# Weights of the second layer loaded in the last batch of the first, products of the identity in three gaps of TensorE, and both orders of steps rewritten

## The chip, the core and the metric

The kernel runs on one core of one Trainium2 chip. The metric is the device time of one execution in microseconds. In the texts PE is TensorE, DVE is VectorE, ACT is ScalarE, POOL is GpSimd and SP is SyncE, whose only work is to issue transfers. ACT issues transfers as well.

## The reference

Two layers are applied one after the other to an input of 16 batches, each of 512 tokens by 128 features. Each layer normalizes its input and adds to it an attention part and a part with experts.

```
x  = L0_attn_x                                    # 16 x 512 x 128
xn = layernorm(x)
x  = x + attention_0(xn) + soft_experts(xn)       # layer 1
xn = layernorm(x)
x  = x + attention_1(xn) + routed_experts(xn)     # layer 2
```

- attention_0 has 16 heads of 8 features, a latent of 128 for keys and values, a rotary part of 32, and a causal softmax.
- soft_experts forms logits of the tokens against 8 x 64 slot vectors (themselves normalized), softmaxes them over the tokens for what goes into the slots and over the slots for what comes out, and runs 8 experts (128 to 512 to 128, gelu).
- attention_1 has 16 heads of 64 features and a causal softmax over the 512 tokens of a batch.
- routed_experts has 16 experts and one shared one, each 128 to 128 to 128 with silu. Of the 16 the best 8 by sigmoid score are kept for each token.

## The kernel before

Each layer is one block of the program (`layer0`, `layer1`), in which every engine has a stream of its own. Between the blocks all engines meet. The intermediate x goes through a tensor in HBM, `x1_scratch`.

Within a layer the work of a batch is cut into named steps: `norm`, `scale` and `xnT` (layer norm and turning it), `q`, `k`, `r`, `v`, `max` (scores for the row maximum, a masked product), `turn_max`, `exp` (scores again, with the maximum taken off by a row in the product), `values`, `turn_rows` and so on, and for the experts `logits_s`, `logits_c`, `dispatch`, `slots`, `hidden`, `expert_out`, `combine` in the first layer and `gate_in`, `up_in`, `hw`, `down` in the second. A table written out by hand, `ORDER0` or `ORDER1`, says in which order the steps of one batch stand among those of the next and the last (the number behind the name: `("norm", 1, 0)` is the norm of the next batch). `layer0_program` and `layer1_program` repeat the table for each batch, and every engine walks through the same list and does its part of each step. An engine never goes on to a later step while it waits in an earlier one.

PE writes into eight banks of PSUM. Four are a ring for everything (`ps_any`, handed out by `Banks`, which gives a step the bank that was filled longest ago, so that a step waits until the step that held the bank has been emptied), the others hold the scores for the exponential (`ps_exp`), the sums over values (`ps_out`) and in the second layer the sums of the exponentials (`ps_sum`).

At the start of the first layer SP issues 18 loads of weights and constants and then x of the first batch, and ACT issues w1, b1, w2 and eight loads of b2. DVE and POOL normalize the slot vectors (`slot_n`), PE turns them into `snT`, and only then does the list of steps begin. At the start of the second layer SP issues 11 loads and x, ACT issues seven. ACT and DVE split every weight into a high and a low half in 16 bits (`low_weights`): four before the first step, and the three expert matrices `w_g`, `w_u`, `w_d` together before the first `gate_in`, for which PE waits:

```
                if at == first_expert:
                    pe.wait_ge(weights_lo, len(split_in) + len(split_late))
                    pe.wait_ge(late_loaded, all_late)
```

In the second layer a causal mask is added to scores by a product of its own behind each piece of scores: 128 columns by `ident_h` and `mask_h` in `exp`, and two halves of 64 columns for each of two heads by `later_h` and `ident_2` in `max`. `max`, `values` and `sums` use part of the array at a time (64 rows, 64 columns, 32 columns), other products all of it.

## Time and profile before

| what | value |
|---|---|
| median of 3 runs | 3098.85 us (3097.3 to 3101.01) |
| profiled execution | 3096.49 us, its span 3094.8 us |
| clock granted to TensorE, mean of the span | 0.984 of full |
| first layer, from the first instruction to the last product | 0 to 1157 us |
| second layer | 1161 to 3095 us |

The span runs from the first to the last instruction, and 1.7 us lie around it. A full clock of TensorE is 2.4 GHz, a granted clock of 0.5 is 1.2 GHz. PE is busy for 93% of the span, but this figure is made of pipelined products with modelled ends, so that short gaps between groups of products do not show in it.

### The profile page before, as it was taken

The numbers are of one execution on the slowest core, as the hardware profiler recorded it, in microseconds if no ns is written. First come the engines' busy times: TensorE is split into PE (matmuls) and PEld (weight loads), VectorE is DVE, ScalarE is ACT, GpSimd is POOL, SyncE is SP. The second block draws the span as 40 slices with busy tenths as digits, with TensorE's granted clock in tenths as the row PEclk, the third lists the DMA queues.
The fourth block names the chain that finished last, engine by engine and source line by source line (L and its number), as shares of the span: only waits on it lengthen the run. The fifth ranks groups of instructions, "written<-read, shape, count | busy, mean of one in ns | idle before, by whom it ended". The sixth has DMA issues, their size and how long they took to land.

```text
span 3094.8 us, 63911 instructions
## 1 busy us (share of the span) xinstructions
PE 2884.3 (93%) x23492; PEld 1512.2 (49%) x23492; DVE 2310.2 (75%) x4199; ACT 1802.6 (58%) x3771; POOL 1314.4 (42%) x1223
## 2 busy tenths in 40 slices
PE   3999999999999984999999999999999999999997
PEld 1555555555555551444444444444444444444443
DVE  4777777777777755778878878878778778778874
ACT  2777766667776763555555555555555555555543
POOL 0433333333333321544544554554554554544543
PEclk8999999999999996999999999999999999999998
DMA  4222222222222214444444444444444444444442
GB/s 112 59 57 54 53 72 68 54 59 56 59 52 61 68 29 131 117 119 115 120 122 116 120 122 115 121 121 115 123 119 116 122 120 115 126 117 115 118 120 69
DMA packets 271910, 297.70 MB, mean 96 GB/s; under 512 B 30832, under 2 KB 235760, under 8 KB 271088
## 3 DMA queue, kind: packets, MB, share of 16 engines
q1 hardware_dynamic: 249936, 276.88, 35.2%
q10 hardware_dynamic: 21664, 16.73, 1.7%
q8 instruction: 189, 3.10, 0.4%
q14 instruction: 121, 0.99, 0.1%
HBM read 141.46 MB, written 25.69 MB: 54 GB/s over the span
## 4 chain that ended last, share of the span: by engine, by line
PE 51%; DMA 3%; DVE 3%; issue 2%; SPq 2%; ACT 1%; POOL 0%; DVEq 0%; ACTq 0%; POOLq 0%
PE l_ps_out L1643 8%; PE l_ps_any L1543 6%; PE l_ps_any L1545 6%; PE l_ps_any L1544 6%; PE l_ps_any L1668 5%; PE l_ps_exp L1626 4%; PE l_ps_any L1675 4%; PE l_ps_exp L1628 4%; PE l_ps_any L1601 3%; DMA l_y_rec<-rec_scratch 2%; PE l_ps_sum L1654 2%; PE l_ps_exp L1630 2%; SPq L1173 1%; DVE l_neg_max L1466 1%; PE l_ps_any L1606 1%
## 5 line engine op out<-in xcount | busy, mean ns | idle before, releaser
L1260 POOL TENSOR_TENSOR l_hid<-l_hid,l_spread 128x512 f32<-128x512 f32 x256 | 327.9, 1281 | 655.1 <-DVE l_hid L1495 480.3
L1347 ACT ACTIVATE l_probs<-l_ps_exp 128x512 f32<-128x512 f32 x640 | 376.8, 595 | 211.4 <-PE l_ps_exp L1630 201.0
L673 DVE TENSOR_REDUCE neg_max<-ps_any 128x1 f32<-128x384 f32 (+3 forms) x704 | 411.0, 634 | 115.7 <-PE ps_any L800 113.7
L536 ACT ACTIVATE probs<-ps_exp 128x512 f32<-128x512 f32 x640 | 352.1, 607 | 41.5 <-PE ps_exp L815 28.4
L455 POOL TENSOR_SCALAR_AFFINE_SELECT probs<-probs 128x512 f32<-128x512 f32 x256 | 160.0, 637 | 458.9 <-ACT probs L536 457.4
L1466 DVE TENSOR_REDUCE l_neg_max<-l_ps_any 128x2 f32<-128x768 f32 (+2 forms) x384 | 316.1, 862 | 35.4 <-PE l_ps_any L1606 34.4
L1626 PE MATMUL l_ps_exp<-l_q_a,l_k_a 128*128 128x512 f16 (+3 forms) x1024 | 306.4, 300 | 10.3 <-DMA l_q_b<-l_max_row 6.5
L1643 PE MATMUL l_ps_out<-l_probs,l_v 128*64 128x512 f32 (+3 forms) x2048 | 303.9, 439 | 0.7 <-ACT l_yT L1322 0.7
L1499 DVE TENSOR_TENSOR l_hw<-l_hid,l_hw 128x512 f16<-128x512 f32 x272 | 257.9, 953 | 60.2 <-ACT l_hw L1330 60.0
L1353 ACT ACTIVATE l_hid<-l_ps_any 128x512 f32<-128x512 f32 x272 | 162.4, 597 | 236.3 <-PE l_ps_any L1545 217.9
L1628 PE MATMUL l_ps_exp<-l_q_b,l_k_b 65*128 65x512 f16 (+3 forms) x1024 | 295.2, 300 | 0.0
L798 PE MATMUL ps_any<-k_st,q_st 120*128 120x128 f16 (+3 forms) x1024 | 254.4, 304 | 30.6 <-DMA k_st<-stack_scratch 12.1
L1242 POOL TENSOR_TENSOR l_key_sum<-l_probs 128x768 f32<-128x768 f32 x128 | 232.4, 1815 | 0.0
L815 PE MATMUL ps_exp<-q_st,k_st 121*128 121x512 f16 (+3 forms) x1024 | 223.9, 302 | 4.7 <-DMA q_st<-max_row 4.2
L1489 DVE SCALAR_TENSOR_TENSOR l_hid<-l_hid,l_ps_any 128x512 f32<-128x512 f32 x272 | 185.3, 681 | 51.7 <-ACT l_hid L1353 47.4
L1495 DVE TENSOR_TENSOR l_hid<-l_ps_any,l_hid 128x512 f32<-128x512 f32 x272 | 186.3, 685 | 41.5 <-PE l_ps_any L1545 33.6
L1643 PEld LDWEIGHTS l_ps_out<-l_probs,l_v 128*64 128x64 f32 x2048 | 135.7, 136 | 162.4 <-issue 139.0
L1330 ACT ACTIVATE l_hw<-l_hid 128x512 f16<-128x512 f32 x272 | 167.3, 621 | 78.6 <-POOL l_hid L1260 62.4
L1630 PE MATMUL l_ps_exp<-l_mask_h,l_ident_h 128*128 128x128 bf16 x1024 | 212.3, 219 | 0.0
L1247 POOL TENSOR_TENSOR l_key_sum<-l_key_sum,l_probs 128x512 f32<-128x512 f32 x128 | 171.6, 1341 | 70.0 <-ACT l_probs L1347 63.0
L800 PE MATMUL ps_any<-mask_h,ident_h 128*128 128x128 bf16 x1024 | 196.6, 221 | 0.0
L1322 ACT ACTIVATE l_yT<-l_ps_out 128x512 f32<-128x512 f32 x128 | 76.1, 595 | 202.4 <-PE l_ps_out L1643 202.4
(262 smaller groups left out, 6731.5 us busy)
## 6 DMA issues: line engine op xcount, KB each, us to landing
l_spread<-route_scratch SPq DMA_DIRECT2D x128, 512.0 KB, 4.7
l_q_a<-l_q_hi SPq DMA_DIRECT2D x256, 128.0 KB, 2.4
l_y_rec<-rec_scratch SPq DMA_DIRECT2D x128, 256.0 KB, 4.3
l_q_b<-l_q_lo SPq DMA_DIRECT2D x128, 128.0 KB, 2.4
l_k_a<-l_k_hi SPq DMA_DIRECT2D x128, 128.0 KB, 3.2
l_k_a<-l_k_lo SPq DMA_DIRECT2D x128, 128.0 KB, 2.8
l_k_b<-l_k_hi SPq DMA_DIRECT2D x128, 128.0 KB, 2.9
q_st<-rot_hi SPq DMA_DIRECT2D x64, 128.0 KB
```

The lines of the kernel that those rows point to most:

```text
L536: nc.scalar.activation(probs[:, n % 2, u], ps_exp[:, (10 * g + u) % 3], ACT.Exp, scale=float(HD0 + DR) ** -0.5).then_inc(exp_done.sem, 1)
L673: nc.vector.tensor_reduce(neg_max[:, n % 2, heads[0]:heads[0] + k, t], src, AX.X, ALU.max, negate=True).then_inc(drained["dve"], 1)
L798: pe.matmul(out, q_st[0:K_MAX0, n % 2, h, t * P:t * P + P], k_st[0:K_MAX0, n % 2, h, 0:w], start=True, stop=False)
L1242: nc.gpsimd.tensor_tensor(s[:, :, P:T], u[:, 0:2, P:T], u[:, 2:4, 0:3 * P], ALU.add).then_inc(added.sem, 1)
L1260: nc.gpsimd.tensor_tensor(at, at, spread[:, c % 3, n % SPREAD], ALU.mult).then_inc(weighted.sem, 1)
L1347: nc.scalar.activation(probs[:, n % 2, u], ps_exp[:, (5 * p + u) % ST_BANKS], ACT.Exp, scale=float(HD1) ** -0.5).then_inc(exp_done.sem, 1)
L1466: ins = nc.vector.tensor_reduce(maxima[:, :, q, t], scores[:, :, c:c + (t + 1) * P], AX.X, ALU.max, negate=True)
L1499: nc.vector.tensor_tensor(hw[:, k % HW_SLOTS, 1], hid[:, k % HID_SLOTS], hw[:, k % HW_SLOTS, 0], ALU.subtract).then_inc(hw_ok.sem, 1)
L1626: pe.matmul(out, k_a[:, g % 2, h, k * P:k * P + P], q_a[:, g % 2, h, k * P:T], start=True, stop=False)
L1628: pe.matmul(out, k_b[0:K_B, g % 2, h, k * P:k * P + P], q_b[0:K_B, g % 2, h, k * P:T], start=False, stop=False)
L1630: ins = pe.matmul(out[:, 0:P], ident_h[:], mask_h[:], start=False, stop=True)
L1643: ins = pe.matmul(ps_out[HD1 * r:HD1 * r + HD1, k * P:T], v[:, k, h * HD1:h * HD1 + HD1], probs[:, n % 2, u, c:c + T - k * P], start=(k == ...
```

## The change

- **Start.** SP issues x of the first batch first, then 8 loads. The other ten go onto ACT's queue, ahead of w1, b1 and w2. The eight loads of b2 are issued by SP at the third `load_heads`. The slot vectors are normalized and turned in a new step `snT`, which stands eight steps ahead of the first logits. POOL, not DVE, clears `v_aug`. `squares` shares its place with `slot_n`.
- **Between the layers.** A class `Early` holds memory that both layers use (`stage`, `ident`, `bias`, `x_in` of the second layer). 14 loads of second-layer weights are issued by ACT in the last batch of the first layer, one ahead of each of the last 14 exponentials, and x of batch 0 by SP at the last `load_heads`. ACT no longer waits for the last store of the first layer at the end of its block. Only w_u, w_d and w_out are loaded at the start of the second layer. The splitting of weights is spread over steps: w_d, above all, only at the first `hw`. POOL clears `k_b`.
- **Products of the identity.** PE multiplies the identity by itself (128 x 128, 32 bits, into a bank that the next user overwrites) 8 times when its first loads have come, 24 times ahead of the first `max`, and 20 times at the start of the second layer.
- **Masks of the second layer.** The masks of an `exp` or `max` step with two pieces are added by one product over both pieces.
- **Sums of the second layer.** The first `sums` of a set of four waits for the reciprocals of the set just before it, not of the one before that.
- **Both tables** `ORDER0` and `ORDER1` are rewritten. They hold the same steps.

```diff
+SPIN_START, SPIN_STACK, SPIN_TURN = 8, 24, 20
 ORDER0 = (
-    ("exp", 0, 0, 4), ("logits_s", 0, 0), ("exp", 0, 0, 5), ("exp", 0, 0, 6), ("soft_s", 0, 0),
+    ("exp", 0, 0, 1), ("attnT", -1, 0), ("exp", 0, 0, 2), ("max", 0, 1, 5), ("exp", 0, 0, 3), ("max", 0, 1, 6),
...
+    first = min(steps.index(x) for x in (("logits_s", 0, 0), ("logits_c", 0, 0)))
+    return steps[:first - 8] + [("snT", 0, 0)] + steps[first - 8:]
...
+            sp.dma_start(x_in[:], a["L0_attn_x"][0].rearrange("(t p) d -> p t d", p=P)).then_inc(x_loaded.sem, 16)
             for dst, src in loads:
                 sp.dma_start(dst, src).then_inc(loaded, 16)
...
+                if name == "load_heads" and (b, n) == (0, 2):
+                    for dst, src in b2_loads:
+                        sp.dma_start(dst, src).then_inc(late_loaded, 16)
+                if name == "load_heads" and (b, n) == (batches - 1, G - 1):
+                    sp.wait_ge(stored.sem, stored.at(0, 16))
+                    sp.dma_start(early.x_in[:], x1_dram[0].rearrange("(t p) d -> p t d", p=P)
+                                 ).then_inc(early.x_loaded.sem, 16)
...
+            for dst, src in act_loads:
+                act.dma_start(dst, src).then_inc(act_loaded, 16)
             act.dma_start(w1_in, a["L0_ffn_w1"].rearrange("e d h -> d e h")).then_inc(w1_loaded, 16)
...
+                    k = len(early.loads) - (G - n) * len(EXP0) + u if b == batches - 1 else -1
+                    if k >= 0:
+                        act.dma_start(*early.loads[k]).then_inc(early.loaded, 16)
                     nc.scalar.activation(probs[:, n % 2, u], ps_exp[:, (10 * g + u) % 3], ACT.Exp,
...
-            act.wait_ge(stored.sem, stored.at(batches, 0))
...
+            def spin(count):
+
+                for _ in range(count):
+                    pe.matmul(ps_exp[:, 2, 0:P], ident[:], ident[:], start=True, stop=True)
+
+            spin(SPIN_START)
...
+                if at == first_max:
+                    spin(SPIN_STACK)
+                    pe.wait_ge(prep, 3)
...
+                if at == first_hw:
+                    act.wait_ge(down_loaded, 32)
+                    high_weights(split_late[1:])
+                    act.wait_ge(weights_lo, len(split_in) + 1)
+                if name == "xnT" and b == 0:
+                    high_weights(split_in[4:])
...
-                        ins = pe.matmul(out[:, 0:P], ident_h[:], mask_h[:], start=False, stop=True)
-                    ins.then_inc(exp_full.sem, 1)
+                    out = ps_exp[:, m % ST_BANKS].rearrange("p (x q) -> p x q", q=P)
+                    pe.matmul(out[:, diagonals([c for r, k, c in EXP1[step[3]]])], ident_h[:],
+                              mask_h[:, 0:len(EXP1[step[3]])], start=False, stop=True
+                              ).then_inc(exp_full.sem, 1)
...
-                    if j == 0 and p >= 2 * SET:
-                        pe.wait_ge(rec_ok.sem, rec_ok.at(p // SET - 1, 0))
+                    if j == 0 and p >= SET:
+                        pe.wait_ge(rec_ok.sem, rec_ok.at(p // SET, 0))
```

The order of instructions shows three places. The first is DVE at the start of the program, before the change (`slot_nat`, `slot_n`, `snT` belong to the slot vectors, `BN_STATS` is the norm of the first batch):

```order
L572 MEMSET v_aug 128x2048
L573 MEMSET k_st 32x4096
L577 ISA squares,slot_ss<-slot_nat 128x128
...
L580 TENSOR_SCALAR slot_sm<-slot_ss 128x4
L583 SCALAR_TENSOR_TENSOR slot_n<-slot_nat,slot_r,slot_gamma 128x128 x4
L585 CAST ident_h<-ident 128x128
...
L591 TENSOR_TENSOR snT<-ps_any,snT 128x512
L603 BN_STATS stats<-x_in 128x6 x4
```

and after it, with the same engine:

```order
L601 MEMSET k_st 32x4096
L636 BN_STATS stats<-x_in 128x6 x4
L640 BN_AGGR mv<-stats 128x2 x4
L642 TENSOR_SCALAR var_eps<-mv 128x4
L648 TENSOR_SCALAR xn<-x_in,mv,rstd 128x128 x4
L626 CAST ident_h<-ident 128x128
L627 CAST mask_h<-mask 128x128
...
L607 ISA slot_n,slot_ss<-slot_nat 128x128
...
L610 TENSOR_SCALAR slot_sm<-slot_ss 128x4
L613 SCALAR_TENSOR_TENSOR slot_n<-slot_nat,slot_r,slot_gamma 128x128 x4
L618 SCALAR_TENSOR_TENSOR snT<-ps_any,snT 128x512
```

The norm of the first batch now stands ahead of all work on the slot vectors, which begins at row 34 of this engine's stream where it began at row 3. The second place is DVE at the start of the second layer, before the change (`l_w_...` are the low halves of split weights, `l_score` begins the choice of experts):

```order
L1362 MEMSET l_k_b 64x4096
...
L1369 CAST l_ident_h<-l_ident 128x128
...
L1379 SCALAR_TENSOR_TENSOR l_w_kvd<-l_probs,l_w_kvd 128x128
...
L1379 SCALAR_TENSOR_TENSOR l_w_kvu<-l_probs,l_w_kvu 128x2048
L1433 BN_STATS l_stats<-l_x_in 128x6 x4
...
L1386 SCALAR_TENSOR_TENSOR l_xn_p<-l_ps_any,l_xn_p 128x512
L1395 TENSOR_SCALAR l_score<-l_th 128x64
...
L1379 SCALAR_TENSOR_TENSOR l_w_g<-l_yT,l_w_g 128x2176
L1379 SCALAR_TENSOR_TENSOR l_w_u<-l_hw,l_w_u 128x2176
L1379 SCALAR_TENSOR_TENSOR l_w_d<-l_hid,l_w_d 128x2176
```

and after it:

```order
L1415 MEMSET l_ones_in 128x128
...
L1489 BN_STATS l_stats<-l_x_in 128x6 x4
...
L1495 TENSOR_SCALAR l_var_eps<-l_mv 128x4
...
L1434 SCALAR_TENSOR_TENSOR l_w_q<-stage,l_w_q 128x1024
L1501 SCALAR_TENSOR_TENSOR l_shift<-l_mv,l_rstd 128x4
L1434 SCALAR_TENSOR_TENSOR l_w_kvu<-stage,l_w_kvu 128x2048
L1422 CAST l_ident_h<-ident 128x128
...
L1441 SCALAR_TENSOR_TENSOR l_xn_p<-l_ps_any,l_xn_p 128x512
L1434 SCALAR_TENSOR_TENSOR l_w_g<-stage,l_w_g 128x2176
L1450 TENSOR_SCALAR l_score<-l_th 128x64
...
L1434 SCALAR_TENSOR_TENSOR l_w_u<-l_hw,l_w_u 128x2176
...
L1434 SCALAR_TENSOR_TENSOR l_w_d<-l_yT,l_w_d 128x2176
```

Four splits and the clearing of `l_k_b` stood ahead of the norm, now none does, and the three expert matrices stand apart from each other. The third place is PE inside the second layer, one `exp` and one `max` step with two pieces each, before the change:

```order
L1626 MATMUL l_ps_exp<-l_q_a,l_k_a 128x384
L1628 MATMUL l_ps_exp<-l_q_b,l_k_b 128x384
L1630 MATMUL l_ps_exp<-l_mask_h,l_ident_h 128x128
L1626 MATMUL l_ps_exp<-l_q_a,l_k_a 128x128
L1628 MATMUL l_ps_exp<-l_q_b,l_k_b 128x128
L1630 MATMUL l_ps_exp<-l_mask_h,l_ident_h 128x128
...
L1601 MATMUL l_ps_any<-l_k_hi,l_q_hi 128x384 x2
L1606 MATMUL l_ps_any<-l_ident,l_later_h 128x64 x4
L1601 MATMUL l_ps_any<-l_k_hi,l_q_hi 128x128 x2
L1606 MATMUL l_ps_any<-l_ident,l_later_h 128x64 x4
```

and after it:

```order
L1705 MATMUL l_ps_exp<-l_q_a,l_k_a 128x384
L1707 MATMUL l_ps_exp<-l_q_b,l_k_b 128x384
L1705 MATMUL l_ps_exp<-l_q_a,l_k_a 128x128
L1707 MATMUL l_ps_exp<-l_q_b,l_k_b 128x128
L1710 MATMUL l_ps_exp<-l_mask_h,l_ident_h 128x2x128
...
L1678 MATMUL l_ps_any<-l_k_hi,l_q_hi 128x384 x2
L1678 MATMUL l_ps_any<-l_k_hi,l_q_hi 128x128 x2
L1685 MATMUL l_ps_any<-l_ident,l_later_h 128x2x64 x4
```

The two mask products behind the pieces of one `exp` step have become one over 2 x 128 columns, and the eight small ones of a `max` step four over 2 x 64 columns.

## Rows read from the trace of the kernel before

**Rows 1.** The page: busy time of each engine

```profile
PE 2884.3 (93%) x23492; PEld 1512.2 (49%) x23492; DVE 2310.2 (75%) x4199; ACT 1802.6 (58%) x3771; POOL 1314.4 (42%) x1223
```

**Rows 2.** Busy time by stretch: length, then busy us and count of each engine, clock granted to PE as a share, DMA share, GB/s

```profile
52.60:76.00 23.40, 17.60 (x101) 9.51 (x102) 17.75 (x25) 10.04 (x15) 0.64 (x1) 0.69 0.15 33
110.00:1100.00 990.00, 935.28 (x8981) 550.83 (x8980) 739.56 (x1661) 695.21 (x1682) 351.24 (x377) 1.00 0.24 60
1157.20:1189.00 31.80, 0.04 (x1) 0.00 (x0) 10.68 (x27) 4.81 (x8) 1.14 (x2) 0.53 0.53 198
1189.00:1211.40 22.40, 9.05 (x38) 3.77 (x38) 13.70 (x28) 10.70 (x12) 0.00 (x0) 0.58 0.42 100
1211.40:1230.00 18.60, 15.63 (x88) 6.05 (x89) 13.69 (x20) 6.02 (x12) 5.08 (x4) 0.75 0.09 24
1230.00:3000.00 1770.00, 1740.69 (x12957) 854.89 (x12955) 1396.11 (x2202) 972.34 (x1807) 881.85 (x764) 1.00 0.47 119
```

**Rows 3.** Timeline of the start: start, us, engine, line, what [idle before <- releaser]

```profile
0.80 0.40 SPq L381 DMA_DIRECT2D ident<-in_ident  x1
...
11.14 4.93 SPq L381 DMA_DIRECT2D w_kr<-in_L_attn_W_k_rope  x3
16.11 1.02 SPq L388 DMA_DIRECT2D x_in<-in_L_attn_x  x1
...
23.13 0.29 DVE L577 CUSTOM_DVE_ANT_0 squares<-slot_nat 128x128 f32<-128x128 f32 x1 [15.69 <-DMA w_kr<-in_L_attn_W_k_rope]
...
29.57 0.86 DVE L603 BATCH_NORM_STATS2 stats<-x_in 128x6 f32<-128x128 f32 x4
...
34.76 0.60 ACT L469 ACTIVATE xnT<-ps_any 128x512 f32<-128x512 f32 x1 [5.91 <-PE ps_any L738]
...
52.62 0.29 PE L798 MATMUL ps_any<-k_st,q_st 120*128 120x128 f16 x1 [11.23 <-DMA k_st<-stack_scratch]
```

**Rows 4.** Transfers of the first 60 us: size of one and median us to landing

```profile
x_in<-in_L_attn_x SPq DMA_DIRECT2D x1, 256.0 KB, 7.5
```

**Rows 5.** PE's waits from 200 to 1000 us: us in total, times, longest

```profile
PE ps_any L798 <- ACT hT L553: 8.4, 22, 0.5
PE ps_any L738 <- ACT y_un L543: 8.1, 11, 0.7
PE ps_any L738 <- DVE xn L615: 8.1, 12, 0.7
```

**Rows 6.** PE's waits from 1300 to 3000 us

```profile
PE l_ps_any L1601 <- DVE l_neg_max L1466: 6.7, 9, 1.7
PE l_ps_exp L1626 <- DMA l_q_b<-l_max_row: 6.5, 5, 1.6
```

**Rows 7.** Timeline between the layers

```profile
1158.10 0.37 ACTq L567 DMA_DIRECT2D x_scratch<-x  x1
...
1161.75 3.47 DVE L1362 MEMSET l_k_b<- 64x4096 f16 x1 [3.69 <-PEq L205]
```

**Rows 8.** The chain of waits between the layers: start, us, what

```profile
1182.00 2.29 DVE l_w_kvu L1379
...
1202.33 1.91 ACT l_w_g L1279
1204.27 2.42 DVE l_w_g L1379
```

**Rows 9.** PE's waits between 1189 and 1230 us

```profile
PE l_ps_any L1543 <- DVE l_w_d L1379: 9.7, 1, 9.7
```

**Rows 10.** Timeline of PE around one set of value products in layer two

```profile
2009.11 0.22 PE L1630 MATMUL l_ps_exp<-l_mask_h,l_ident_h 128*128 128x128 bf16 x1
2009.25 2.38 PE L1643 MATMUL l_ps_out<-l_probs,l_v 128*64 128x512 f32 x16
2011.56 0.39 PE L1543 MATMUL l_ps_any<-l_xn_p,l_w_u 128*128 128x512 f16 x1
```

**Rows 11.** DVE's reciprocals of the sums, all 64

```profile
L1478 DVE RECIPROCAL l_rec<-l_ps_sum x64: 886/918/958, 1291.5 to 3070.4; 128x128 f32<-128x128 f32 x64
```

More of the change, by code:

```diff
@@ L383, in _ @@
                 n = which[0]
-                if name == "load":
+                if name == "load" and b:
                     if b:
@@ L472, in _ @@
                 n = which[0]
+                if name == "snT":
+                    nc.scalar.activation(snT[:, 0], full(act, "snT0"), ACT.Copy).then_inc(snT_hi, 1)
                 if name in ("xnT", "ckv"):
@@ L596, in low_part @@
                                                       op0=ALU.mult, op1=ALU.subtract)
-            for name, b, *which in program:
+            for at, (name, b, *which) in enumerate(program):
                 n = which[0]
+                if at == after_scale:
+                    dve.wait_ge(loaded, all_loaded)
+                    dve.wait_ge(act_loaded, all_act)
+                    nc.vector.tensor_copy(ident_h[:], ident[:]).then_inc(prep, 1)
+                    nc.vector.tensor_copy(mask_h[:], mask[:]).then_inc(prep, 1)
+                if name == "snT":
+                    slots_normed()
+                    bank = full(dve, "snT0")
+                    dve.wait_ge(snT_hi, 1)
+                    low_part(bank, snT, 1.0).then_inc(drained["dve"], 1)
                 if name == "norm":
@@ L955 @@
+    ("values", 0, 7), ("max", 1, 1, 0), ("max", 1, 1, 1), ("sums", 0, 7),
 )
@@ L1523, in _, with spin @@
         def _(pe):
-            pe.wait_ge(loaded, all_loaded)
-            pe.wait_ge(prep, 12)
-            pe.wait_ge(weights_lo, len(split_in))
+            def spin(count):
+                for _ in range(count):
+                    pe.matmul(ps_exp[:, ST_BANKS - 1, 0:P], ident[:], ident[:], start=True, stop=True)
+            spin(SPIN_TURN)
+            pe.wait_ge(early.loaded, early.all)
             def bank(name):
```

416 lines of the change are left out of this document (235 added, 181 removed).

## The prediction

> **What bounds the kernel now.** I read the page first, then busy time by stretch, then PE's waits in each stretch, and last the timeline and the chain of waits where a stretch is not full. The page gives PE 93% and no other engine over 75% [rows 1]. By stretch this is two full layers with gaps around them: PE is busy for 935 of the 990 us from 110 to 1100, and for 1741 of the 1770 us from 1230 to 3000, at the full clock in both [rows 2]. In these two stretches time can come only from fewer products, from closer products, or from PE's waits. The waits are small: in 800 us of the first layer 8.4 us for a bank that the gelu holds, 8.1 for `y_un`, 8.1 for the normalized x [rows 5]; in 1700 us of the second 6.7 for row maxima and 6.5 for the row of maxima that is brought by a transfer [rows 6].
>
> The gaps are different. At the start the reader should see three rows: x is issued only at 16.11, behind 18 other issues; DVE waits 15.69 us for the last weight and begins with the slot vectors at 23.13, and the norm begins at 29.57; the copy of xnT starts at 34.76, and the first scores at 52.62 [rows 3]. Between the layers PE does nothing from 1157.2 to 1189.0 while transfers run [rows 2], then works at a granted clock of 0.58, and waits 9.7 us for the last of the expert weights [rows 2, 9].
>
> **Start.** x is now issued at 0.80, where `ident` was. Its transfer took 7.5 us among others [rows 4], so it is there by 8.3 at the latest. The norm to the copy of xnT took 34.76 - 29.57 = 5.2 us [rows 3]. DVE would allow the copy at 13.5 or before. ACT must first issue 13 transfers: at the 0.40 us of `ident` this is 5.2 us, at the 4.93/3 = 1.64 us of `w_kr` it is 21 us [rows 3]. The issues that were slow stood behind a full queue, so I take 1.0 us for each of six short rotary pieces and 0.6 for the rest, 10 us in all, with a table load and the last landing at 14. The gain at xnT is 34.8 - 14 = 21 us, with bounds 12 and 26. From xnT to the first scores lie the same products, splits and transfers as before, 52.6 - 34.8 = 17.9 us [rows 3]; loads of w1 and w2 now run into them. I take 20.
>
> Given back: the slot work, on DVE from 23.13 to 29.57 [rows 3], comes later, in a stretch in which DVE is busy for 17.8 of 23.4 us and PE for 17.6 [rows 2]. What is not waiting in it is about 4 us of DVE. Also eight issues of b2 stand in SP's queue before the second row of maxima, 8 x 0.4 = 3.2 us [rows 3]. Hidden both cost nothing, on the path 7. I take 2.5. The 24 products of the identity fill a gap of 11.23 us [rows 3]; the stretch behind it ran at a clock of 0.69 [rows 2]. If the clock stays full, at most 17.6 x 0.31 = 5 us come back. 24 products of 128 columns in 32 bits end long before the stacks come, so I take 1.5. **Start: -20 + 2.5 - 1.5 = -19.**
>
> **Last batch of the first layer.** 14 issues on ACT, 14 x 0.4 = 5.6 us by the row of `ident`, each behind a wait for scores and ahead of an exponential. ACT is busy for 695 of 990 us [rows 2], so most of it is covered; without cover PE waits for a bank of scores each time. **+2**, bounds 0 and 5.6.
>
> **Between the layers.** Without the wait for the store the block ends some 2 us sooner: it is issued at 1158.10, and DVE's first instruction of the next layer starts at 1161.75 [rows 7]. Say DVE starts at 1159.8. Short clears 0.5, norm 1.6. ACT meanwhile issues 5 transfers (2.5) and converts four weights (3.2), which lasts until 1165.0. Scaling x (1.65), turning (1.1), the high half of w_g ahead of the copy (1.91, as in [rows 8]), copy and low half (1.3) give 1171 for what stood at 1191.6. That is 20.5 us. Now w_g's low half stands before the choice of experts, 2.42 us [rows 8], which leaves 18. The wait of 9.7 us for three matrices [rows 9] shrinks to w_u's conversion, 1.91 + 2.4 = 4.3 [rows 8]: 5.4 more. w_d's 4.3 comes later, on an ACT and a DVE that are busy for 6.0 and 13.7 of 18.6 us [rows 2]: half of it on the path, 2. The clock in 1189 to 1230 was 0.58 and 0.75 over 24.7 us of busy PE [rows 2], at most 7.7 us; the 20 products end some 5 us after the block starts and the next product is due about 8 us after it, so the clock may hold. I take 3.5, since DVE is nearly full too. **-18 - 5.4 + 2 - 3.5 = -25**, bounds -17 and -32.
>
> The Trainium skill (DMA: Bandwidth & Descriptors, "Issuing engines are not separate DMA queues") says that transfers of all engines share the same 16 DMA engines and that several issuers save only issue time. By it alone the start would gain little. The trace agrees in so far as DVE waits until 23.13 us for the last small load [rows 3]; but what PE waits for is the order of the bytes, and x and the weights of the first products come first now.
>
> **Steady part, first layer.** Same steps, other order. Distances in "us of products" below are counted from the two tables, a column as a cycle of 2.4 GHz (four in 32 bits), as are the changes of the array's shape. In the new table `values` (32 columns of the array), `r` and `expert_out` are more often neighbours: 23 changes between parts of the array and all of it per batch against 26. Such a change costs about 0.1: a mask product at 2009.11 ends its 0.05 of columns at 2009.16, and the value products behind it start at 2009.25 [rows 10]. Three fewer in each of 16 batches are 5 us. The wait for the normalized x (8.1 in 800 us, 0.7 a batch) should go, since 3.3 us of products now stand between `scale` and `xnT`, where 1.0 stood; `y_un` likewise (0.86 before, 1.9 now for the worst). `hidden` banks are reused after 1.45 us three times, as tight as before. In full that is 5 + 2 x 0.7 x 15 = 26 us. A new order opens waits that I can't see, so I take half. **-12**, bounds -26 and +10.
>
> **Steady part, second layer.** Masks: 8 products per pair of heads become 5, and 32 per group 20, with the same columns. What a product costs beyond its columns these rows don't show; I put it at 2 ns, so that 384 + 768 fewer are worth 2 us, with nothing and 10 us as ends. Changes of the array's shape go from 58 to 61 a batch, +5 us. The row of maxima has 3.8 us of products before its use at the tightest place against 2.3: some of the 6.5 us [rows 6]. **-1**, bounds -12 and +16.
>
> The skill (TensorEngine Tiling (Array Packing), "Key Properties") says that a change of tiling mode drains the engine. The gap of 0.09 us in rows 10 agrees. By that rule alone the tables would give -5 and +5, together nothing.
>
> **Sum.** -19 + 2 - 25 - 12 - 1 = -55 on the profiled execution's 3096.5 is 3041.5. The median of the runs shown is 2.4 above that execution, so I say **3044**.
>
> **Rivals.**
> - *The tables do more than I count.* An order chosen for this program takes out most remaining waits in both layers: 26 in the first, 12 in the second. 3044 - 14 - 11 = 3019. For it: every wait of rows 5 is of the kind an order can move. Against it: the tightest reuses of banks are alike in both.
> - *The tables cost.* `sums` of a new set waits for the reciprocals of the set before. They take 2 x 0.92 us [rows 11] on DVE, and only 4.3 us of products stand between the last `sums` of one batch and the first of the next, where 10.2 stood. DVE has a reduction of about 1.3 us before them, so some 3.3 us are needed on an idle DVE; a lag of 2 us costs 1 us a batch. With the 5 us of array changes, 13 above my sum, and no gain in the first layer, 12: 3069.
> - *The gaps give half.* Loads and stacks of the start collide, and DVE with its 14 us of conversions sets the pace between the layers. -9 and -13: 3066.
> - *Slower.* The same wait for reciprocals, with DVE late by 5 us: PE then loses 3.9 us twice a batch. It decides from 55/30 = 1.8 us for each of 30 sets. The other set has 14.5 us of products, so both would have to fail; DVE is busy for 1396 of 1770 us [rows 2], which leaves room: above 3105.
> - *The identity does nothing* for the clock: +5, inside my range.
>
> **How the numbers follow.** My forecast 0.55 (its own range 3028 to 3058), better tables 0.19, costly tables 0.11, half the gaps 0.12, slower 0.03. The range takes all but the ends: 3018 to 3068. A measurement of this kernel tells about 0.2% (6 us) from no change. The gaps alone give some 40 us, so faster 0.96, same 0.01, slower 0.03.
>
> **What would show it.** xnT's copy at 12 to 17 us and first scores at about 33; a granted clock of 1.0 from 33 to 56 if the products of the identity work. No transfer of weights on the path after the first layer's end; the turning of x within 9 us of the block's start; a wait of PE for w_u under 5 us, none for w_d. In the stretches, PE's idle share below 5.5% in the first layer, and rows for xn and `y_un` gone. I am wrong if PE waits for `l_rec`, if ACT issues its loads slowly at the start, or if the step `snT` shows as a hole.

## The result, and the profile after

The changed kernel takes **3175.78 us** (median of 4 runs, 3173.21 to 3181.64); the kernel before, 3098.76. The ratio is 1.0251, 95% interval 1.0233 to 1.0268: slower by 77 us where I forecast 55 us less. The profiled execution took 3174.8 us, with a span of 3173.1. Groups 0 to 3 below are the four groups of four heads that a batch has in either layer, each with its own `turn_max`; "the row" of a group is the row of maxima that this step brings into the stacks by a transfer of SP.

The page's line on busy time (the one of [rows 1]) and the costliest line of products of scores in the second layer:

```profile
PE 2920.2 (92%) x22444; PEld 1516.9 (48%) x22444; DVE 2223.2 (70%) x4199; ACT 1789.7 (56%) x3771; POOL 1321.8 (42%) x1226
...
L1705 PE MATMUL l_ps_exp<-l_q_a,l_k_a 128*128 128x512 f16 (+3 forms) x1024 | 309.4, 308 | 83.8 <-DMA l_q_b<-l_max_row 83.6
```

PE sat 83.6 us before L1705 until a transfer of 4 KB had landed; the page's chain of waits has this transfer second, with 5% of the span. Busy time by stretch, columns as in [rows 2], says where that is:

```profile
110.00:1100.00 990.00, 921.20 (x8874) 549.59 (x8873) 727.00 (x1651) 691.31 (x1667) 347.29 (x373) 1.00 0.23 60
1157.00:1189.00 32.00, 17.53 (x98) 10.93 (x96) 18.67 (x57) 13.88 (x20) 4.64 (x3) 0.79 0.44 136
...
1230.00:3000.00 1770.00, 1675.61 (x11236) 798.49 (x11236) 1256.55 (x2114) 905.25 (x1711) 836.96 (x723) 0.98 0.45 112
```

The gap between the layers is filled as forecast. In the second layer, PE is busy for 1675.6 of 1770 us where it was for 1740.7, and its granted clock is 0.98 where it was 1.00 [rows 2]. PE's waits in this stretch (from 1230 us; [rows 6] begin at 1300), and from 200 to 1000 us, as in [rows 5]:

```profile
PE l_ps_exp L1705 <- DMA l_q_b<-l_max_row: 77.0, 29, 7.6
PE l_ps_any L1678 <- DVE l_neg_max L1530: 10.9, 45, 0.3
```

```profile
PE ps_any L840 <- DMA k_st<-stack_scratch: 16.0, 15, 1.7
PE ps_any L772 <- POOL disp_s L470: 12.7, 11, 1.2
PE ps_exp L857 <- DMA q_st<-max_row: 3.8, 7, 0.8
PE ps_any L772 <- ACT y_un L573: 2.6, 11, 0.2
```

The waits that I wanted gone from the first layer are gone or smaller (`xn`, `y_un`), and two transfers and `disp_s` stand in their place. Split at starts of the same product in both traces (us; the second column less the first is what each part cost or gave):

| part, from and to | before | after | change |
|---|---|---|---|
| start to the second batch's first `turn_max` | 132.6 | 125.8 | -6.8 |
| from there to that of the last batch, 14 batches of layer one | 956.0 | 965.8 | +9.8 |
| to the issue of the last x1 store | 69.5 | 69.5 | 0 |
| to the gate products of layer two's second batch | 127.1 | 103.6 | -23.5 |
| 14 batches of layer two | 1624.5 | 1715.3 | +90.8 |
| the rest | 185.1 | 193.1 | +8.0 |
| sum | 3094.8 | 3173.1 | +78.3 |

A batch of the second layer takes 122.5 us instead of 116.0; that is where the time went. The timeline of SP's queue and of PE around one such wait shows how:

```profile
1827.26 0.33 SPq L1237 DMA_DIRECT2D rec_scratch<-l_rec  x1
1830.57 1.25 SPq L1246 DMA_DIRECT2D l_y_rec<-rec_scratch  x2
1831.93 1.00 SPq L1229 DMA_DIRECT2D l_spread<-route_scratch  x2
1833.00 0.57 SPq L1213 DMA_DIRECT2D l_q_b<-l_max_row  x1
...
1840.12 0.39 PE L1705 MATMUL l_ps_exp<-l_q_a,l_k_a 128*128 128x512 f16 x1 [3.72 <-DMA l_q_b<-l_max_row]
```

SP brings the reciprocals in and two spreads (`l_spread`) within 2.4 us, and the row right behind them. The view of transfers, for 1832.9 to 1841 us (size, time from issue to landing):

```profile
l_spread<-route_scratch SPq DMA_DIRECT2D x1, 512.0 KB, 7.3
...
l_q_b<-l_max_row SPq DMA_DIRECT2D x1, 4.0 KB, 7.1
```

The 4 KB land about when the last of the large transfers ahead of them does: in batches 2 to 16, 0.25 us behind the last spread on average. Before, the same place of the program read:

```profile
1819.94 0.33 SPq L1201 DMA_DIRECT2D rec_scratch<-l_rec  x1
1821.70 1.25 SPq L1210 DMA_DIRECT2D l_y_rec<-rec_scratch  x2
1823.06 0.53 SPq L1193 DMA_DIRECT2D l_spread<-route_scratch  x1
1829.04 0.57 SPq L1177 DMA_DIRECT2D l_q_b<-l_max_row  x1
```

There the transfers had 6 us to drain, and one 512 KB piece fewer stood there. Mean time to landing of the 16 rows of group 1, each from its issue to the last update of its semaphore: 2.20 us before, 7.13 after. "Landing" below is this mean, unless a row is shown.

### The profile page after: what moved, and what is told of

It is laid out like the page before. It is cut to its first block, busy times and chain, and to the rows that moved or that the text cites. A ratio compares the mean times of both kernels' runs of the same rounds, so it can differ in the third digit from the quotient of the medians.

```text
span 3173.1 us, 61841 instructions
## 1 busy us (share of the span) xinstructions
PE 2920.2 (92%) x22444; PEld 1516.9 (48%) x22444; DVE 2223.2 (70%) x4199; ACT 1789.7 (56%) x3771; POOL 1321.8 (42%) x1226
## 4 chain that ended last, share of the span: by engine, by line
PE 42%; DVE 8%; DMA 6%; issue 3%; ACT 2%; SPq 2%; ACTq 0%; DVEq 0%
PE l_ps_out L1724 7%; DMA l_q_b<-l_max_row 5%; PE l_ps_any L1611 5%; PE l_ps_any L1749 5%; PE l_ps_any L1613 4%; PE l_ps_any L1612 4%; PE l_ps_exp L1705 4%; PE l_ps_any L1758 3%; PE l_ps_exp L1707 3%; PE l_ps_any L1678 3%; DVE l_neg_max L1530 2%; PE l_ps_exp L1710 1%; PE l_ps_sum L1735 1%; DVE l_rec L1542 1%; SPq L1246 1%
## 5 line engine op out<-in xcount | busy, mean ns | idle before, releaser
L1302 POOL TENSOR_TENSOR l_hid<-l_hid,l_spread 128x512 f32<-128x512 f32 x256 | 354.9, 1387 | 738.3 <-DVE l_hid L1559 734.8
L1400 ACT ACTIVATE stage<-l_ps_exp 128x512 f32<-128x512 f32 x640 | 373.4, 597 | 320.6 <-PE l_ps_exp L1710 307.2
L1705 PE MATMUL l_ps_exp<-l_q_a,l_k_a 128*128 128x512 f16 (+3 forms) x1024 | 309.4, 308 | 83.8 <-DMA l_q_b<-l_max_row 83.6
L1724 PE MATMUL l_ps_out<-stage,l_v 128*64 128x512 f32 (+3 forms) x2048 | 304.8, 440 | 0.8 <-ACT stage L1400 0.8
L1563 DVE TENSOR_TENSOR l_hw<-l_hid,l_hw 128x512 f16<-128x512 f32 x272 | 194.0, 723 | 157.7 <-ACT l_hw L1383 157.3
L1707 PE MATMUL l_ps_exp<-l_q_b,l_k_b 65*128 65x512 f16 (+3 forms) x1024 | 283.2, 308 | 0.0
L1284 POOL TENSOR_TENSOR l_key_sum<-stage 128x768 f32<-128x768 f32 x128 | 231.7, 1810 | 0.0
L1724 PEld LDWEIGHTS l_ps_out<-stage,l_v 128*64 128x64 f32 x2048 | 136.1, 137 | 174.4 <-issue 153.3
L1289 POOL TENSOR_TENSOR l_key_sum<-l_key_sum,stage 128x512 f32<-128x512 f32 x128 | 163.1, 1274 | 83.4 <-ACT stage L1400 76.4
L1705 PEld LDWEIGHTS l_ps_exp<-l_q_a,l_k_a 128*128 128x128 f16 x1024 | 101.8, 99 | 193.6 <-DMA l_q_b<-l_max_row 99.3
L1749 PE MATMUL l_ps_any<-l_hw,l_w_d 128*128 128x512 f16 x816 | 187.0, 380 | 0.0
```

Of the source, the lines that this page charges most:

```text
L1284: nc.gpsimd.tensor_tensor(s[:, :, P:T], u[:, 0:2, P:T], u[:, 2:4, 0:3 * P], ALU.add).then_inc(added.sem, 1)
L1302: nc.gpsimd.tensor_tensor(at, at, spread[:, c % 3, n % SPREAD], ALU.mult).then_inc(weighted.sem, 1)
L1400: nc.scalar.activation(probs[:, n % 2, u], ps_exp[:, (5 * p + u) % ST_BANKS], ACT.Exp, scale=float(HD1) ** -0.5).then_inc(exp_done.sem, 1)
L1705: pe.matmul(out, k_a[:, g % 2, h, k * P:k * P + P], q_a[:, g % 2, h, k * P:T], start=(c == 0), stop=False)
L1707: pe.matmul(out, k_b[0:K_B, g % 2, h, k * P:k * P + P], q_b[0:K_B, g % 2, h, k * P:T], start=False, stop=False)
L1724: ins = pe.matmul(ps_out[HD1 * r:HD1 * r + HD1, k * P:T], v[:, k, h * HD1:h * HD1 + HD1], probs[:, n % 2, u, c:c + T - k * P], start=(k == ...
```

## Experiments

**1. Two spreads behind the row.** In `ORDER1` of the changed kernel:

```diff
-    ("spread_in", 0, 4),
...
-    ("spread_in", 0, 5),
...
     ("turn_max", 0, 1),
+    ("spread_in", 0, 4), ("spread_in", 0, 5),
```

> The changed kernel with the two steps spread_in(0,4) and spread_in(0,5) moved behind turn_max(0,1) in the second layer's table; PE, ACT, DVE and POOL keep their order, only the order of SP's transfers changes. Theory A (the 4 KB row of maxima stands behind four large transfers that SP issued just before it): its time to landing for group 1 falls from 7.1 us in the middle to 2 to 4, PE's wait for it in the second layer falls from 84 us to under 15, and the full clock comes back; 3176 less 15 batches times 5 to 6.5 gives 3080 to 3100. Theory B (the new table uses the row too soon after it is turned, whatever stands before it): the wait stays and the time is 3176 within 8. Theory C (the new wait of sums for the reciprocals, or the merged masks, is what costs): also 3176 within 8.

Measured: 3076.04 us, ratio to before 0.9933 (0.9918 to 0.9948), 100 us less than the changed kernel and a little better than theory A's band. Landing 2.55 us, a batch of the second layer 116.12 us. PE's wait in the second layer, by the same view as above:

```profile
PE l_ps_exp L1705 <- DMA l_q_b<-l_max_row: 19.4, 16, 1.8
```

Theories B and C fall, since no other step moved. Two steps of SP, on which no product waits for long, decide between slower by 2.5% and faster by 0.7%.

**2. One of them.** The same with `("spread_in", 0, 5)` alone.

> The changed kernel with spread_in(0,5) alone moved behind turn_max(0,1); spread_in(0,4), 512 KB, and the two copies of the reciprocals before it stay ahead. Theory A: the row waits for one large transfer less, lands some 2.3 us sooner, at 4 to 5.5 us, so of the wait of 3.7 us in a batch 1 to 2 stay: 3176 less 15 times 2 to 3.5 gives 3120 to 3145. If the queue is not the reason, 3176 within 8.

Measured: 3110.84 us, 1.0041 (1.0026 to 1.0056). Landing 4.73 us, batch 118.32 us, wait 39.8 us. One 512 KB piece is 2.4 us of landing (7.13, 4.73) and the second one 2.2 (4.73, 2.55); the time fell by 65 us where I had worked out 31 to 56, so it missed the band by 9.

**3. The cause put into the kernel before.** The two steps ahead of `("turn_max", 0, 1)` in its own table.

> The kernel before, with spread_in(0,4) and spread_in(0,5) moved to stand right ahead of turn_max(0,1), and nothing else changed. Theory A: the row of group 1 now lands after 5 to 7 us where it took 1.7 to 3.6, its use is as near as ever, so PE waits 2 to 5 us more in each batch: 3099 plus 30 to 80 gives 3130 to 3180. Theories B and C: no change, 3099 within 8.

Measured: 3097.09 us, 1.0001 (0.9992 to 1.001). A clear miss of theory A's band, and the most useful run. SP's timeline:

```profile
1820.96 1.25 SPq L1210 DMA_DIRECT2D l_y_rec<-rec_scratch  x2
1822.32 1.00 SPq L1193 DMA_DIRECT2D l_spread<-route_scratch  x2
1828.31 0.58 SPq L1177 DMA_DIRECT2D l_q_b<-l_max_row  x1
```

The order in the queue is that of the changed kernel, but the large pieces are issued 5 to 7 us ahead of the row and have drained (landing 2.33 us). What differs is when SP is let go: it waits for the reciprocals' copy out, and in the changed kernel that is issued 5.7 us ahead of the row, here 9.1. So theory A needs a second half: SP must also be held until just before the row.

**4. Both halves in the kernel before.** The same, with `("rec", -1, 1)`, DVE's reciprocals, moved back behind `("max", 0, 1, 3)`, where the new table has them.

> The kernel before with the same two steps ahead of turn_max(0,1) as before_two_ahead, which cost nothing, and now also rec(-1,1) moved back behind max(0,1,3), where the changed table has it. Theory A2: SP is held at the reciprocals until 1 to 3 us before the row, the row of group 1 lands after 5 to 7 us instead of 2.3, and each batch takes 3 to 5 us more: 3145 to 3180. Theory A1: no change against before_two_ahead, 3099 within 8.

Measured: 3231.04 us, 1.0435 (1.0417 to 1.0452): 134 us slower for three steps moved, more than I had said. SP's timeline, the row's landing and PE's wait:

```profile
1863.17 1.25 SPq L1210 DMA_DIRECT2D l_y_rec<-rec_scratch  x2
1864.53 1.00 SPq L1193 DMA_DIRECT2D l_spread<-route_scratch  x2
1865.59 0.57 SPq L1177 DMA_DIRECT2D l_q_b<-l_max_row  x1
```

```profile
l_q_b<-l_max_row SPq DMA_DIRECT2D x1, 4.0 KB, 9.3
```

```profile
PE l_ps_exp L1626 <- DMA l_q_b<-l_max_row: 107.2, 14, 8.5
```

The mechanism is shown in both kernels. The row shown lands after 9.3 us, the 16 of group 1 after 8.08 on average. Two things make it dearer here. The row is used sooner than in the new table (2.3 us of products against 3.8, by the prediction's count). And it is issued later: SP, still busy with the transfers ahead, issues it 1.9 us behind the product that turns the maxima, where the kernel before takes 0.66 and the changed one 0.8 (means of batches 2 to 16).

**5. Only the reciprocals earlier, in the changed kernel.** `("rec", -1, 1)` moved to the head of `ORDER1`.

> The changed kernel with one step of DVE moved: rec(-1,1), the reciprocals of the last set of a batch, goes from behind the third product of maxima to the head of the second layer's table, so that SP, which is held at the copy of the reciprocals, is free sooner. The four large transfers keep their places ahead of turn_max(0,1). Theory A2 (the row waits because SP is held up to 1 us before the row and then issues four large transfers in one go): the transfers leave some 3 us or more ahead of the row, it lands after 2 to 5 us instead of 7.1, and the time falls from 3176 to 3080 to 3120. Theory A1 (their order in the queue alone decides, whenever they are issued): 3176 within 8.

Measured: 3152.16 us, 1.0176 (1.0161 to 1.0191); neither band. At the place shown, the copy out came 6.6 us ahead of the row instead of 5.7, but SP was let go from it only 3.7 us later (3.3 before this edit), and so the last spreads still left 0.9 to 1.5 us ahead:

```profile
1821.51 0.36 SPq L1237 DMA_DIRECT2D rec_scratch<-l_rec  x1
1825.23 1.25 SPq L1246 DMA_DIRECT2D l_y_rec<-rec_scratch  x2
1826.59 1.00 SPq L1229 DMA_DIRECT2D l_spread<-route_scratch  x2
1828.08 0.57 SPq L1213 DMA_DIRECT2D l_q_b<-l_max_row  x1
```

A spread is issued 0.6 us ahead of that small copy out, which then takes its turn behind it. Landing 6.05 us, batch 121.1 us. That fits large transfers that left only a little sooner; moving the reciprocals was the weak lever.

**6. All rows first.** As run 1, with `("rec_in", -1, 2)` and `("rec_in", 0, 1)` behind their rows as well.

> As two_behind, and the two copies of reciprocals that still stand just ahead of a row, rec_in(-1,2) and rec_in(0,1), moved behind turn_max(0,1) and turn_max(0,3). By theory A2 groups 1 and 3 then land after 1.7 to 2 us (2.6 and 3.9 in two_behind), the wait of 19 us for the row falls to under 8, and the time is 3076 less 8 to 16: 3060 to 3068. If what is left of the wait has another reason, 3076 within 6.

Measured: 3076.80 us, 0.9937 (0.9921 to 0.9953). Every row now lands after 1.8 us, and PE's wait for it is gone, as forecast; but the time is that of run 1, outside the band of 3060 to 3068. The waits of its second layer:

```profile
...
PE l_ps_any L1678 <- DVE l_neg_max L1526: 8.2, 15, 0.6
PE l_ps_any L1678 <- DVE l_hid L1559: 5.5, 14, 0.6
PE l_ps_any L1678 <- DVE l_k_lo L1441: 5.0, 7, 1.3
...
PE l_ps_exp L1705 <- DMA l_q_b<-l_max_row: 0.4, 1, 0.4
```

Against run 1, the waits for `l_neg_max` L1526 (8.2) and `l_k_lo` (5.0), both of DVE, are new. It seems that what was left of the wait for the row had covered them; no run tests this.

**7. The second layer's table of before, in the changed kernel.**

> The changed kernel with the second layer's table of before. All that the change does outside this table stays: loads, start, first layer's table, merged masks, the wait of sums for the reciprocals, the products of the identity. If the table alone costs (A or B), a batch of the second layer takes 115.5 to 116.5 us again, not 122.4, and the time is 3176 less 15 times 6.3 less some 5 of the tail, 3065 to 3085. If the wait of sums or the merged masks cost (C), the batch stays above 118 and the time above 3110.

Measured: 3068.99 us, 0.9908 (0.9891 to 0.9924), batch 115.77 us. The table alone is the loss; the loads, the merged masks and the wait of `sums` are not. With its rows first the new table is at 116.08, still 0.3 us a batch behind the old.

**8. The first layer's table of before, in the changed kernel.**

> The changed kernel with the first layer's table of before. The batch of the first layer takes 68.99 us in the changed kernel and 68.29 before. If the table is the reason, the batch is back at 68.3 and, if the table also is why the gain of 18 us at the first maxima has shrunk to 7 by the second batch, the first batch keeps 15 to 18: 3176 less 10 to 21 gives 3155 to 3166. If slot work, loads or the POOL's part are the reason, the batch stays at 69.0 and the time within 6 of 3176.

Measured: 3186.95 us, 1.0291 (1.0275 to 1.0306): slower than the changed kernel, outside both bands. With the old table a batch takes 69.48 us; the same table took 68.29 in the kernel before, with the same issues of SP at the same distances from the row. In the transfers around one row of group 1 (697 to 701 us, and 694 to 698 before) the two, shown in this order, differ in one packet:

```profile
q8 instruction: 1, 0.02, 1.8%
...
q_st<-max_row SPq DMA_DIRECT2D x1, 4.0 KB, 3.0
```

```profile
q_st<-max_row SPq DMA_DIRECT2D x1, 4.0 KB, 1.7
```

It is an instruction fetch of 16 KB beside the 32 of the row; it started 0.7 us behind the row's issue. These fetches belong to PE: between 200 and 500 us of this run, PE's count of loads of weights, products and semaphore waits at a fetch, modulo 256, lay between 177 and 251 in all 21 cases. The whole program agrees. The kernel before has 23492 products, as many loads and 1534 semaphore waits of PE, which is 189.5 times 256, and the changed one 22444, 22444 and 1554, which is 181.4 times. The pages of the two have, in this order:

```profile
q8 instruction: 189, 3.10, 0.4%
```

```profile
q8 instruction: 181, 2.97, 0.4%
```

A batch of the first layer has 1283 such instructions, 5 times 256 and 3 more, so a fetch keeps its place in the batch, and its transfer neighbour, for many batches. In batches 2 to 16 of run 8 a fetch starts 0.6 to 1.2 us behind every row of group 1; in the kernel before none starts within 5 us of one. A batch of the second layer has 1749 (before) or 1605 of them, far from a multiple of 256, so there the fetches wander. That made theory F of the next runs.

**9. The phase moved in the kernel before.** 28 products of the identity ahead of the first maxima, 112 instructions of PE:

```diff
+                if at == first_max:
+                    for _ in range(28):
+                        pe.matmul(ps_exp[:, 2, 0:P], ident[:], ident[:], start=True, stop=True)
```

> The kernel before with 28 products of the identity in the gap of 11 us ahead of the first maxima, nothing else. Theory F (found in the traces: every 256th instruction of PE falls together with a 16 KB packet of queue 8, an instruction fetch; a batch of the first layer is 1283 instructions of PE, 5 times 256 and 3, so the fetches keep their place in the batch, and a row of maxima issued 0 to 1.5 us ahead of one lands 1 to 1.5 us late): 28 products are 112 instructions, which moves the fetches to where the changed kernel with the old first table has them, 0.5 to 1.3 us behind the row of group 1. That row lands after 2.6 to 3.2 us instead of 1.7, a batch of the first layer takes 68.9 to 69.5 us instead of 68.3, and the time is 3098 plus 8 to 18. Rival G (the first layer is slower in the changed kernel by its other placements in memory or by its loads): the batch stays at 68.3, and the time within 5 of 3098. By either theory the clock of the first maxima should rise if the products do what they are for, which would give back at most 5.

Measured: 3116.35 us, 1.0057 (1.0042 to 1.0072). The row of group 1 lands after 2.94 us (1.73 before) and the batch takes 69.45 us. PE's waits from 200 to 1000 us now begin with

```profile
PE ps_exp L819 <- DMA q_st<-max_row: 10.7, 17, 1.0
```

of which [rows 5] had nothing. A fetch starts 0.6 to 1.2 us behind the row of group 1 in all of batches 2 to 16, as in run 8. 14 batches by 1.16 us are 16 of the 18 us; the other 2 are at the start, where the first maxima come at 53.9 instead of 52.6 us.

**10. The phase moved back.** As run 8, without the 8 and 24 products of the start:

```diff
-SPIN_START, SPIN_STACK, SPIN_TURN = 8, 24, 20
+SPIN_START, SPIN_STACK, SPIN_TURN = 0, 0, 20
```

> As old_order0 (3187 us), without the 8 and 24 products of the identity at the start; those between the layers stay. Theory F: 128 fewer instructions of PE bring the fetches back to 0.4 to 0.9 us behind the row of group 2, as in the kernel before; the row of group 1 lands after 1.7 us instead of 3.0, a batch of the first layer takes 68.2 to 68.6 us instead of 69.48, and the time falls by 12 to 18 to 3169 to 3175, less or more what the products give or cost in the clock of the start (0 to 5). Rival G: the batch stays at 69.5 and the time within 5 of 3187.

Measured: 3160.80 us, 1.0203 (1.0185 to 1.022), 26 us less than run 8, where theory F had 12 to 18. Landing of group 1's row 1.75 us and batch 68.40 us, both as it said; the batches are 15 of the 26 us. The first maxima come at 32.1 instead of 35.2 us, 3 more; the rest is spread over the other parts and is not explained. Rival G falls with runs 9 and 10.

**11. The best of both.** As run 7, again without the products of the start.

> As old_order1 (3069 us), without the 32 products at the start. Theory F: with the new first table the fetches leave the landing of the stacks ahead of group 0, where they stand now (0.9 us behind its row), and come 0.3 to 1.2 us behind the rows of groups 2 and 3 instead. Those two have more slack, so a batch of the first layer takes 68.0 to 68.6 instead of 68.79, which gives 3069 less 3 to 11. If the products hold the clock at the start, up to 5 us come back as a loss. Rival G: 3069 within 4.

Measured: **3055.10 us, 0.9861 (0.9846 to 0.9876)**, the fastest kernel of this study, 43 us under the one before and 3 under theory F's band. The first layer takes 68.05 us a batch, the second 115.62. The phase is better, not perfect: the rows of groups 2 and 3 now land after 2.5 and 2.8 us, those of groups 0 and 1 after 1.7, and from 200 to 1000 us PE has no wait for a row in its list.

**12. The slots in the gap.** As run 7, `snT` ahead of the first maxima:

```diff
-    return steps[:first - 8] + [("snT", 0, 0)] + steps[first - 8:]
+    return steps[:first] + [("snT", 0, 0)] + steps[first:]
```

with `first` the place of the first `max`.

> As old_order1 (3069 us), with the slot vectors' step snT moved ahead of the first product of maxima, into the 9.5 us in which DVE waits for the stacks. In the changed kernel DVE does them at 53.98 to 57.75 and PE waits 4.3 us. If that chain is on the path, the second batch's turn_max comes 4 to 7 us sooner and the time is 3062 to 3065. If DVE's conversion of w1 (4.42 us) and the late clock set the pace there, it is within 2 of 3069, and the new place may cost a late first maximum.

Measured: 3067.06 us, 0.99 (0.9886 to 0.9915), within 2 of run 7. The first maxima come at 39.6 instead of 34.5 us, the second batch's `turn_max` at 125.5 instead of 126.0, so the slot work is paid in either place. This run shows one thing more. Its 24 products of the identity end where the first maxima start, and PE has the full clock behind them (timeline, then busy time by stretch, its clock the third number from the end):

```profile
33.09 6.63 PE L760 MATMUL ps_exp<-ident 128*128 128x128 f32 x48
39.56 0.22 PE L840 MATMUL ps_any<-k_st,q_st 120*128 120x128 f16 x1
```

```profile
39.70:52.00 12.30, 7.64 (x64) 4.51 (x61) 9.33 (x14) 4.85 (x4) 0.00 (x0) 1.00 0.10 25
```

In run 7 the granted clock is 0.78 from 34.5 to 46 us and 0.51 from there to 63. So the maxima come 5 us later and nothing is lost by the second batch: PE's wait of 4.3 us for the slot vectors further on is gone, and the clock is higher. The shares of the two are not separated, and no run has this order without the products.

**13. No product of the identity at all, ten, and separate masks.** Each is run 11 with one thing changed: `SPIN_TURN = 0`; `SPIN_STACK = 10`; the second layer's masks added one by one, as before.

> As old_order1_no_start (3055 us), also without the 20 products of the identity between the layers, so that no product of the identity is left. If they hold the clock, the stretch behind the first layer's end runs slower and up to 7 us are lost: 3058 to 3062. If they do nothing, as at the start, 3055 within 4; the 80 instructions that PE no longer carries also move the fetches of the second layer, whose batches are no multiple of 256 instructions, so nothing is expected from that.

> As old_order1_no_start, with 10 products (40 instructions of PE) ahead of the first maxima. Theory F, worked out by shifting that trace's fetches by 40 instructions: they move to 0.1 us behind or 0.7 us ahead of the row of group 2, away from the stores and the row of group 3 (0.8 us behind now, 2 us ahead then) and to 2 us behind the row of group 0. The batch of the first layer stays at 68.0 or falls to 67.7, 3050 to 3057. By a theory in which more products of the identity are what costs (the 28 and the 32 alike), a third of their cost comes back: 3059 to 3063.

> As old_order1_no_start, with the masks of the second layer added by one product each as before (8 for a pair of heads instead of 5, 32 for a group instead of 20, the same columns). My step put the 1152 fewer products at 2 us of gain in all with ends of 0 and 10: 3055 to 3065, likeliest 3057. If merging the masks had a cost of its own, it is faster than 3052.

Measured: 3058.27 (0.9874, 0.986 to 0.9889), 3062.30 (0.9886, 0.9869 to 0.9902) and 3059.99 us (0.9882, 0.9868 to 0.9897).

Without the 20 products the stretch from the x1 store to the second batch's gate takes 102.6 us, with them 102.8: they give nothing that this can tell. The time itself lies in both bands, and the 3 us more in it are 0.2 us a batch of the second layer.

Ten products missed theory F's band and lie in its rival's. The trace does not side with the rival, though: no row lands late, but the fetch has moved to 11 to 14 us ahead of group 0's row, onto the stacks of that group, which SP issues 12.9 and 12.4 us ahead. PE's wait for stacks from 110 to 1100 us is 13.3 us in 15 waits where run 11 had 6.6, and the batch 68.29. I had looked at the rows alone. This reading came after the run, and no further run tests it.

Separate masks cost 0.35 us a batch, some 5 us: 115.97 against 115.62. About 0.2 of such a difference can come from elsewhere, as the run without products shows.

## Why the prediction was wrong

**Steady part, second layer: the step that failed.** It put -1 with bounds -12 and +16; measured +90.8 and most of the last +8. Its sentence was "the row of maxima has 3.8 us of products before its use at the tightest place against 2.3". I counted how far the use was and took the landing for a constant, as the kernel before had it. The landing was what the table changed: 7.13 us against 2.20, since SP, held at the reciprocals, issued 1.5 MB (two pieces of 256 KB and two of 512 KB) in the last 2.4 us ahead of the row. From the product to the issue are 0.66 us; with 7.1 to the landing and less 3.8 of distance this leaves 4.0 us of wait a batch, and the wait at 1840.12 is 3.72. The order of SP's queue and the size of each transfer could be read before the run; that SP would be let go so late could be read only in part, from the place of `rec` in DVE's order. The bounds were too narrow for a step whose order I had not followed on SP.

**Rivals.** None named this. The slower one (PE waits for the reciprocals of the set before, through the new wait of `sums`) had its point of decision, but no wait for `l_rec` is in the trace, and run 7 keeps that wait of `sums` and is fast. The reciprocals did matter, by another way: SP waits for them. In *The tables cost*, a lag of 1 us a batch and 5 us that the sum already held are put at 13 us; 16 batches of the lag alone are 16. Either way it stays far below the measurement.

**Start, -19.** The first maxima came 18.1 us sooner (52.6 to 34.5), and xnT's copy at 16.39 us, inside the forecast 12 to 17. The six rotary pieces on ACT's queue, for which the working took 1.0 us each, took 1.50 and 1.42 us for three where they now stand first; that a full queue had slowed them before is not shown. By the second batch's `turn_max`, 6.8 were left (3.6 to 7.0 in the six runs that keep this start and first table). What was "given back" I had sized at 2.5; three waits make up most of it: 1.8 us while ACT converts w1, 2.6 us for DVE's half of it, and 4.3 us for the slot vectors, at a low clock:

```profile
45.64 4.42 DVE L666 SCALAR_TENSOR_TENSOR w<-probs,w 128x4096 f16<-128x4096 f32 x1 [2.21 <-ACT w L502]
45.81 0.34 PE L840 MATMUL ps_any<-k_st,q_st 120*128 120x384 f16 x1 [1.82 <-ACT max_row L556]
...
50.72 0.50 PE L840 MATMUL ps_any<-k_st,q_st 120*128 120x384 f16 x1 [2.58 <-DVE neg_max L706]
...
57.80 1.12 PE L772 MATMUL ps_any<-ident,slot_n 128*128 128x128 f32 x4 [4.34 <-DVE slot_n L613]
```

**Products of the identity, -1.5 and -3.5.** In the changed kernel they did nothing for the clock where it mattered. At the start the first 8 come ahead of the turning of x, whose input DVE has finished by 9.15 us:

```profile
8.04 1.11 DVE L648 TENSOR_SCALAR xn<-x_in,mv,rstd 128x128 f32<-128x128 f32 x4 [1.23 <-POOL rstd L462]
...
12.47 3.44 PE L760 MATMUL ps_exp<-ident 128*128 128x128 f32 x16 [12.47 <-DMA mask<-in_mask]
...
15.75 0.60 PE L772 MATMUL ps_any<-ident,xn 128*128 128x128 f32 x4
```

Without them x is turned at 12.5 instead of 16.3 us, and the first maxima come 3.2 us sooner (run 10 against run 8; 1.6 sooner in run 11 against run 7). The other 24 end at 27.3 us, PE then idles 7.2 us until the first maxima, and from 34 to 40 us it is granted 0.56. That step of the working ("end long before the stacks come") was right; run 12, where no such gap is left, has the full clock. Between the layers 1157 to 1189 has 0.79 with them, and run 13 shows no difference without. The rival "the identity does nothing" had it at +5; it missed that 128 more instructions shift every later fetch. Runs 8 and 10 differ by 26 us in these 32 products alone, 15 of them in the batches of the first layer and 3 at the first maxima.

**Last batch, +2; between the layers, -25.** Measured 0 and -23.5 (-25.1 with the old second table, run 7: 102.0 against 127.1). x was turned 8.4 us behind the first product of the block, and no transfer of weights was waited for:

```profile
1161.10 0.38 ACTq L597 DMA_DIRECT2D x_scratch<-x  x1
...
1161.95 6.33 PE L1591 MATMUL l_ps_exp<-ident 128*128 128x128 f32 x40 [1.71 <-PEq L214]
1170.39 0.63 PE L1605 MATMUL l_ps_any<-ident,l_x_in 128*128 128x128 f32 x4 [2.11 <-ACT l_x_in L1337]
```

Before, 31 us lay between that store [rows 7] and the turning of x at 1189.0; now 9.3. This part of the working held, its clock term aside, and but for a slip: 2.5 and 3.2 us from 1159.8 are 1165.5, not 1165.0.

**Steady part, first layer, -12.** Measured +9.8, just inside the bound of +10. The table is better, but by less than I took: with the fetches at a less harmful place it takes 68.05 us a batch against 68.40 for the old one (runs 11 and 10), 5 us in 14 batches, and 3 us less than the kernel before (68.29). It takes away the waits for `xn` and most of those for `y_un`, and brings one for `disp_s`, which POOL releases: 13.9 us in run 11 and 12.7 in the changed kernel, both from 200 to 1000 us. What turns this -3 into +10 is the phase of the fetches, 68.99 in the changed kernel against 68.05 in run 11, 13 us; no term of mine had it. The six kernels with this first layer and the products of the start take 68.68 to 68.99, the three without them (run 11 and two of run 13) 68.05 to 68.10, so its size is 8 to 13 us in 14 batches.

**Masks, -2.** About -5, inside the ends of 0 and -10; up to 3 of the 5 can have another origin (run 13).

Without its second table and without the products at the start, the change is worth 43 us of the 55 that I forecast (run 11).

## What to carry to other kernels

Where a schedule is reordered, follow the issuing queue as an engine of its own: for each small transfer that something waits for, list what the same queue issues in the microseconds ahead of it, with sizes, and what holds the queue before that. Put the small one first; here that was worth 100 us (run 1). What holds the queue matters as much: the same order cost nothing in run 3. A distance in products says only when a transfer is needed, never when it lands.

Look at the period of a loop in instructions. If it is close to a multiple of the 256 of a fetch, any instruction added ahead of the loop is an experiment on the whole loop, and must be measured as one; it was 1.7% of this one (68.29 to 69.45 us).

## What the runs showed of the hardware

One packet of instructions lengthens a small transfer next to it. I read this from all 17 traces, over the 4 KB rows of batches 2 to 16 of the first layer. Where a 16 KB fetch of PE started up to 1.2 us behind the issue of the row (230 rows), it landed after 2.0 to 3.8 us, 2.7 in the middle. Where no fetch started from 1 us ahead to 2.5 us behind (549 rows), it landed after 1.6 to 2.0 us, 1.7 in the middle. The rows of the second layer show the same where no large transfer stands just ahead of them (the kernel before and runs 6, 7, 11 and 13 without products): 2.1 to 3.6 us in 33 rows beside a fetch, 1.7 to 1.8 in 177 without one. Why 16 KB cost a 4 KB row a microsecond is open.

PE fetches once in 256 of its instructions. A product of the identity counts for four of them (32 stand as 64 products and 64 loads of weights), the turning of a 128 x 128 tile for two.

The Trainium skill (DMA: Bandwidth & Descriptors, "Issuing engines are not separate DMA queues") says that transfers started by different engines run on the same 16 DMA engines and interleave there. It speaks of transfers that a program starts, not of fetches. The late rows agree with fetches sharing these engines too; no run here shows it directly.
